# Shared experts as a loop of four groups of token tiles, with the last choice of experts ahead of it

## The chip, the cores and the metric

The kernel runs on one core of one Trainium2 chip. The metric is the device time in microseconds (us) of that core. Five engines work side by side: PE (matrix products), DVE (vector operations and reductions), ACT (activation functions and copies), POOL (here mainly transfers that go through a list of addresses) and SP (here only issues transfers). They run their own instruction lists and meet only at semaphores.

## The reference, cut to what matters

One transformer layer with adaptive norms: latent attention over 2048 tokens, then a mixture of experts of 32 routed experts, six per token, and two shared ones that every token goes through. The change lies in the second half:

```python
scores = jax.nn.sigmoid(x @ gate_w)
...
_, selected_experts = jax.lax.top_k(masked_scores, K)
weights = jnp.take_along_axis(original_scores, selected_experts, axis=-1)
weights = weights / jnp.sum(weights, axis=-1, keepdims=True)
...
g = jax.lax.ragged_dot(xs, w_gate, group_sizes)
u = jax.lax.ragged_dot(xs, w_up, group_sizes)
d = jax.lax.ragged_dot(jax.nn.silu(g) * u, w_down, group_sizes)
...
expert_out = jnp.sum(out * weights[..., None], axis=1)
shared = jax.nn.silu(x @ sw_gate) * (x @ sw_up) @ sw_down
return (expert_out + shared).reshape(B, S, H)
```

## The kernel before, in words

`attention` fills the first 1730 us and is untouched. `mixture` then works on 16 tiles of 128 tokens, in three stages that follow each other on PE.

**Token tiles.** For each tile PE projects the attention output (L1398), DVE adds it to x (`token_tile`, L1159) and normalizes (L1169), PE turns the tile (L1407), ACT modulates it into `h2T` (L1075), and PE computes the 32 scores (L1417). A choice of experts is made for a group of tiles at once: `choose` (L1179 to L1219) and `count_group` on DVE, `positions` on PE (L1430 to L1436), and `place` on DVE, which writes the list of slots (L1249). `GROUP` sets the groups: tiles 0 to 1, 2 to 7 and 8 to 15. The first two are chosen inside the loop over tiles, one and two tiles after the last tile of the group. When a group's slots stand, POOL scatters the rows of its tiles to the regions of the experts in DRAM, six transfers for each tile (L1050). One group's row of transfers is called a burst below: 12, 36 and 48 of them.

**Shared experts.** 32 units (16 tiles times the two halves of the shared experts), written out one after the other. In a unit PE computes gate and up (`shared_gate`, L1475), ACT the silu (L1103), DVE the product (L1313), PE turns it (`shared_turn`, L1484), ACT copies it (`shared_hidden`, L1109), PE multiplies down (`shared_down`, L1493); after each second unit DVE adds the result to x (L1339). The gate product of unit n+2 is issued ahead of the down product of unit n. The choice of the last group is spread between the first six units; `count_chosen`, `tile_table` (L1253 to L1274), `spread_table` (L1448) and `keep_table` follow up to unit 10. They yield the table that says which expert each of the 128 routed tiles uses; SP waits for it before it loads the first weights (L1008). `weigh_tokens` (L1285 to L1293), seven pieces on DVE, is spread over units 12 to 24.

**Routed experts.** 128 tiles, a loop on every engine with eight tiles in its body: SP loads a tile's weights (L1008, one transfer of 608 KB) and its rows (L1014), PE, ACT and DVE do the same steps as for a unit (L1519 to L1542, product on DVE L1348), POOL scatters the result (L1059). `combine` then adds six rows per token to x (L1611).

```python
GROUP = ((0, 2), (2, 8), (8, 16))
...
for n in range(UNITS):
    shared_turn(n)
    if n + 2 < UNITS:
        shared_gate(n + 2)
    shared_down(n)
```

Of the kernel before, what the change touches and what calls it, by code (L numbers as in the profile page):

```python
# [36 lines left out]
TOPK = 6  # L37
GROUPS = 4
EPG = E // GROUPS
M = 176  # L40
# [830 lines left out]
def mixture(nc, a, x, ident, mod, wov, cbar, routing, weight, slots_dram, ranked_dram):  # L871

    st = ExitStack()
    with st:
# [24 lines left out]
        h2T = sb("h2T", T * D)  # L899
# [71 lines left out]
        folded = sem("folded3")  # L971
        sg_mm = sem("sg_mm3")
# [22 lines left out]
        CREDIT = {r_mm: U, r_used: 2, g_mm: 2, hid_ready: 2, h_mm: 2, h_used: 2, y_mm: U, y_ready: 2}  # L995
# [70 lines left out]
        def _(act):  # L1066
# [32 lines left out]
            def shared_silu(n):  # L1099
                act.wait_ge(sg_mm, n + 1)  # L1100
                if n >= 2:
                    act.wait_ge(s_hid, n - 1)
                act.activation(ex[n % 2][:, :], p_g[n % 2][:, 0:M], ACT.Silu).then_inc(s_silued, 1)  # L1103

            def shared_hidden(n):
                act.wait_ge(sh_mm, n + 1)
                if n >= 2:
                    act.wait_ge(sd_mm, n - 1)
# [44 lines left out]
        def _(v):  # L1153
# [155 lines left out]
            def shared_hid(n):  # L1309
                v.wait_ge(s_silued, n + 1)  # L1310
                if n >= 2:
                    v.wait_ge(sh_mm, n - 1)
                v.tensor_tensor(hid[n % 2][:, :], ex[n % 2][:, :], p_g[n % 2][:, M:2 * M], ALU.mult).then_inc(s_hid, 1)  # L1313

            for n in range(2):
                shared_hid(n)
            for n in range(UNITS):
                if n + 2 < UNITS:
                    shared_hid(n + 2)
                if n == 0:  # L1320
                    scores(END)
                if n == 1:
                    best_groups(END)
                if n == 2:
                    inside_groups(END)
                if n == 3:
                    best_experts(END)
                if n == 4:
                    count_group(END)
                if n == 5:  # L1330
                    place(END)
                if n == 7:
                    tile_table()
                if n == 10:
                    keep_table()
                if n % 2 == 1:
                    t = n // 2
                    v.wait_ge(sd_mm, n + 1)
                    v.tensor_tensor(x[:, t * D:(t + 1) * D], p_y[t % 2][:, 0:D], x[:, t * D:(t + 1) * D],  # L1339
                                    ALU.add).then_inc(s_added, 1)  # L1340
                if n % 2 == 0 and 12 <= n < 12 + 2 * (TOPK + 1):
                    weigh_tokens((n - 14) // 2)
# [41 lines left out]
        def _(pe):  # L1384
# [85 lines left out]
            def shared_gate(n):  # L1470
                t = n // 2
                if n >= 2:
                    pe.wait_ge(s_hid, n - 1)
# [5 lines left out]
            def shared_turn(n):  # L1479
                pe.wait_ge(s_hid, n + 1)  # L1480
                if n >= 2:
                    pe.wait_ge(sh_used, n - 1)
# [4 lines left out]
            def shared_down(n):  # L1487
                t = n // 2
                pe.wait_ge(sh_used, n + 1)
                if n % 2 == 0 and t >= 2:  # L1490
                    pe.wait_ge(s_added, t - 1)
                for k in range(2):
                    last = pe.matmul(p_y[t % 2][:, 0:D], hidT[n % 2][:, k * P:(k + 1) * P],  # L1493
# [3 lines left out]

            pe.wait_ge(ld_ws, 32)
            pe.wait_ge(folded, 2)
            for n in range(2):  # L1500
                shared_gate(n)
            pe.wait_ge(x_used, T)
            for n in range(UNITS):
                shared_turn(n)
                if n + 2 < UNITS:
                    shared_gate(n + 2)
                shared_down(n)
                if n == 4:
                    positions(END)
                if n == 5:  # L1510
                    count_chosen()
                if n == 9:
                    spread_table()
# [43 lines left out]
            pe.wait_ge(s_added, T)  # L1557
# [122 lines left out]
```

## Time and profile before

| what | value |
|---|---|
| median of 3 runs | 2381.33 us (2379.02 to 2386.78) |
| the profiled execution's own time | 2386.19 us |
| its span, first to last instruction | 2384.4 us |
| busy share of the span | PE 90%, DVE 63%, ACT 58%, POOL 56% |
| attention ends, token tiles begin | about 1733 us into the span |
| last addition of the shared experts | 1987.39 us |
| first and last scatter issue (L1050) | 1759.2 and 1936.0 us |
| first transfer of results to be combined lands | about 2334 us |

Times in the rows are microseconds from the start of the span. In a row of the timeline the first number is the start and the second the duration; what stands in brackets is how long the engine sat idle before it, and who released it. "remote" there means that the profile found no event of another engine close before the release. PE and its weight loads (PEld) are listed apart; a product of 32-bit floats shows as two matmuls for each one of the code. `x4` counts instructions that were merged into a row. The granted clock is 1.00 at the higher level of TensorE's clock and 0.50 at the lower.

### The profile page before, as it was taken

How to read it: one execution, taken by the hardware profiler on the slowest of the kernel's cores; microseconds unless marked ns; L12 is line 12 of the kernel's file. 1: busy time of each engine (PE TensorE's matmuls, PEld its weight loads, DVE VectorE, ACT ScalarE, POOL GpSimd, SP SyncE). 2: the span in 40 equal slices, each digit the busy share in tenths (PEclk: the TensorE clock that was granted, in tenths of full speed). 3: DMA queues.
4: the chain of work that ended last, by engine and by line, in shares of the span. 5: the costliest groups of instructions: out<-in, count | busy, mean ns of one | idle time of the engine just before them, and what ended most of it. 6: DMA issues, size and time to landing. Idle time of an engine off the chain costs nothing. (4 is left out here: it accounts for less than half of the span.)

```text
span 2384.4 us, 38677 instructions
## 1 busy us (share of the span) xinstructions
PE 2140.0 (90%) x10554; PEld 1421.9 (60%) x10554; DVE 1511.3 (63%) x3046; ACT 1375.4 (58%) x1927; POOL 1338.5 (56%) x762
## 2 busy tenths in 40 slices
PE   5896999999999999999999999999873659999990
PEld 3643666666666666666666666666553436777760
DVE  4536777777777777777777777777142324555557
ACT  2521677777777777777777777767731214555540
POOL 1001777777777777777777777777725331333330
PEclk8886999999999999999999999999986879999995
DMA  4119990000000000000000000000012244999987
GB/s 158 53 29 370 402 396 7 0 0 0 0 0 0 0 0 0 0 0 0 0 0 0 0 0 0 0 0 1 1 49 81 67 145 142 337 357 343 345 281 249
DMA packets 90336, 227.35 MB, mean 95 GB/s; under 512 B 13198, under 2 KB 46904, under 8 KB 90040
## 3 DMA queue, kind: packets, MB, share of 16 engines
q1 hardware_dynamic: 77240, 195.03, 23.1%
q0 software_dynamic: 10752, 29.72, 3.3%
q10 hardware_dynamic: 2304, 2.10, 0.3%
q8 instruction: 21, 0.34, 0.1%
q14 instruction: 19, 0.16, 0.0%
HBM read 125.52 MB, written 101.28 MB: 95 GB/s over the span
## 5 line engine op out<-in xcount | busy, mean ns | idle before, releaser
L632 POOL TENSOR_TENSOR prob_lo<-prob,prob_hi 128x1024 f16<-128x1024 f32 x512 | 1108.3, 2176 | 435.8 <-ACT prob_hi L651 425.8
L649 ACT ACTIVATE prob<-p_s,prob_scale 128x1024 f32<-128x1024 f32 x512 | 571.4, 1116 | 463.2 <-PE p_s L798 456.9
L684 DVE TENSOR_REDUCE maxes<-p_m 128x1 f32<-128x512 f32 x1024 | 700.7, 691 | 120.5 <-PE p_m L771 103.8
L651 ACT ACTIVATE prob_hi<-p_s,prob_scale 128x1024 f16<-128x1024 f32 x512 | 567.3, 1108 | 0.0
L771 PE MATMUL p_m<-k_hi,q_hi 96*128 96x512 f32 x1024 | 420.5, 414 | 10.4 <-DVE maxes L684 7.7
L798 PE MATMUL p_s<-q_hi,k_hi 97*128 97x512 f32 x1024 | 360.0, 433 | 5.5 <-ACT prob_hi L651 3.9
L798 PE MATMUL p_s<-q_lo,k_hi 97*128 97x512 f32 x1024 | 323.6, 397 | 0.0
L798 PE MATMUL p_s<-q_hi,k_lo 97*128 97x512 f32 x1024 | 323.1, 397 | 0.0
L1059 POOL DMA_INDIRECT ranked_out<-y,dest x128 | 122.8, 959 | 265.7 <-DVE y L1363 258.4
L771 PEld LDWEIGHTS p_m<-k_hi,q_hi 96*128 96x128 f32 x1024 | 195.4, 191 | 91.4 <-DVE maxes L684 34.8
L798 PEld LDWEIGHTS p_s<-q_hi,k_hi 97*128 97x128 f32 x1024 | 171.4, 189 | 121.2 <-issue 67.9
L798 PEld LDWEIGHTS p_s<-q_lo,k_hi 97*128 97x128 f32 x1024 | 192.2, 190 | 41.2 <-issue 1.0
L798 PEld LDWEIGHTS p_s<-q_hi,k_lo 97*128 97x128 f32 x1024 | 192.4, 190 | 40.5
L811 PE MATMUL p_o<-prob_hi,c_hi 128*64 128x512 f16 x1024 | 199.1, 386 | 2.9 <-POOL prob_lo L632 2.9
L811 PE MATMUL p_o<-prob_hi,c_lo 128*64 128x512 f16 x1024 | 196.0, 379 | 0.0
L811 PE MATMUL p_o<-prob_lo,c_hi 128*64 128x512 f16 x1024 | 196.0, 379 | 0.0
L1527 PE MATMUL bank<-w,rT 128*128 128x352 f32 x512 | 175.4, 466 | 2.1 <-ACT rT L1075 2.1
L1050 POOL DMA_INDIRECT expert_rows<-hall,slot x96 | 92.5, 964 | 104.3 <-DVE slot L1249 75.9
L1542 PE MATMUL bank<-w,hidT 88*128 88x256 f32 x512 | 131.9, 379 | 0.9 <-ACT hidT L1131 0.9
L1348 DVE TENSOR_TENSOR hid<-ex,bank 128x176 f32<-128x176 f32 x128 | 43.2, 338 | 134.4 <-ACT ex L1126 124.3
L761 PE MATMUL p_x<-hT,wq 128*96 128x512 f32 x256 | 123.1, 603 | 5.4 <-POOL q_lo L624 3.0
L673 DVE TENSOR_TENSOR q_raw<-p_x,cosq 96x512 f32<-96x512 f32 x64 | 43.9, 687 | 126.3 <-PE p_x L761 126.3
(231 smaller groups left out, 2259.0 us busy)
## 6 DMA issues: line engine op xcount, KB each, us to landing
w<-in_experts SPq DMA_DIRECT2D x128, 608.0 KB
expert_rows<-zeros SPq DMA_DIRECT2D x129, 526.0 KB, 9.1
rows<-expert_rows SPq DMA_DIRECT2D x128, 131.5 KB
got<-ranked_out SPq DMA_DIRECT2D x16, 768.0 KB, 11.1
wqb<-in_wqb SPq DMA_DIRECT2D x16, 341.0 KB, 3.0
x<-in_x SPq DMA_DIRECT2D x1, 2048.0 KB, 8.5
cbar<-in_woT SPq DMA_DIRECT2D x1, 2048.0 KB
ranked_out<-y,dest POOLq DMA_INDIRECT x128
```

Of the source, the lines that this page charges most:

```text
L632: gp.tensor_tensor(prob_lo[s % NB][:, :], prob[s % 2][:, :], prob_hi[s % NB][:, :], ALU.subtract).then_inc(lo_ready, 1)
L649: act.activation(prob[s % 2][:, :], p_s[s % 2][:, :], ACT.Exp, bias=prob_scale[:, :], scale=SCALE)
L651: act.activation(prob_hi[s % NB][:, :], p_s[s % 2][:, :], ACT.Exp, bias=prob_scale[:, :], scale=SCALE).then_inc(p_ready, 1)
L684: v.tensor_reduce(maxes[:, n:n + 1], p_m[n % 2][:, :], AX.X, ALU.max).then_inc(max_used, 1)
L761: last = pe.matmul(p_x[0:KA, :], wq[:, k * KA:(k + 1) * KA], hT[:, k * S + c * QC:k * S + (c + 1) * QC], start=(k == 0), stop=(k == DK - 1))
L771: pe.matmul(p_m[n % 2][:, :], q_hi[half][0:KA, j * P:(j + 1) * P], k_hi[0:KA, kc * QC:(kc + 1) * QC], start=True, stop=True).then_inc(max_ ...
L798: last = pe.matmul(p_s[kt % 2][:, j * QC:(j + 1) * QC], kk[0:KS, keys], qq[half][0:KS, j * QC:(j + 1) * QC], start=(part == 0), stop=(part ...
L811: last = pe.matmul(p_o[j * CP:(j + 1) * CP, :], cc[:, kt * CP:(kt + 1) * CP], pp[:, j * QC:(j + 1) * QC], start=(kt == 0 and part == 0), s ...
L1050: gp.indirect_dma_start(out=slots_dram[0:E * S, :], out_offset=bass.IndirectOffsetOnAxis(ap=slot[:, t * 8 + j:t * 8 + j + 1], axis=0), in_ ...
L1059: gp.indirect_dma_start(out=ranked_dram, out_offset=bass.IndirectOffsetOnAxis(ap=dest[u][:, :], axis=0), in_=y[u][:, :], in_offset=None).t ...
L1527: last = pe.matmul(p_g[u % 2][:, 0:2 * M], rT[u % 2][:, k * P:(k + 1) * P], w[u % U][:, k * 2 * M:(k + 1) * 2 * M], start=(k == 0), stop=( ...
L1542: last = pe.matmul(p_y[u % 2][:, 0:D], hidT[u % 2][:, k * P:(k + 1) * P], w[u % U][0:MH, WIN + k * D:WIN + (k + 1) * D], start=(k == 0), s ...
```

## The change

The groups of tiles become 0 to 5, 6 to 11 and 12 to 15, so the bursts have 36, 36 and 24 transfers, and the first two choices come at tiles 7 and 13 instead of 3 and 9. The choice of the last group, the table of tiles and its spreading stand ahead of the shared experts on DVE and PE. The shared experts become a loop of four trips on PE, ACT and DVE; a trip has eight units (four token tiles). [...] All seven pieces of `weigh_tokens` stand behind the loop on DVE, ahead of the first product of the routed tiles. Semaphores of the stage start with a credit of two, so that a wait in the loop never is for zero. The weights of a tile are loaded by one transfer in both kernels; the diff has no line on them.

```diff
-        UNITS = 2 * T
+        ST = 4
+        UNITS = 2 * ST
-        GROUP = ((0, 2), (2, 8), (8, 16))
+        GROUP = ((0, 6), (6, 12), (12, 16))
...
@@ scalar
+            def copy_h(q, tl):
+                act.wait_ge(sg_mm, q * UNITS + 2 * max(tl - 2, -1) + 4)
+                act.copy(rT[tl % 2][:, :], h2T[:, ds((q * ST + tl) * D, D)]).then_inc(rc_ready, 1)
...
-            for n in range(2):
-                shared_silu(n)
-            for n in range(UNITS):
-                shared_hidden(n)
-                if n + 2 < UNITS:
-                    shared_silu(n + 2)
+            with act.Fori(0, T // ST) as q:
+                for n in range(2):
+                    copy_h(q, n)
+                for n in range(2):
+                    shared_silu(q, n)
+                for n in range(UNITS):
+                    shared_hidden(q, n)
+                    if n % 2 == 0 and n // 2 + 2 < ST:
+                        copy_h(q, n // 2 + 2)
+                    if n + 2 < UNITS:
+                        shared_silu(q, n + 2)
...
@@ vector
+            choose(END)
+            count_group(END)
+            place(END)
+            tile_table()
+            keep_table()
...
-            for n in range(2):
-                shared_hid(n)
-            for n in range(UNITS):
-                if n + 2 < UNITS:
-                    shared_hid(n + 2)
-                if n == 0:
-                    scores(END)
...
-                if n % 2 == 0 and 12 <= n < 12 + 2 * (TOPK + 1):
-                    weigh_tokens((n - 14) // 2)
+            with v.Fori(0, T // ST) as q:
+                for n in range(2):
+                    shared_hid(q, n)
+                for n in range(UNITS):
+                    if n + 2 < UNITS:
+                        shared_hid(q, n + 2)
+                    if n % 2 == 1:
+                        xt = x[:, ds((q * ST + n // 2) * D, D)]
+                        v.wait_ge(sd_mm, q * UNITS + n + 3)
+                        v.tensor_tensor(xt, p_y[n // 2 % 2][:, 0:D], xt, ALU.add).then_inc(s_added, 1)
+            for j in range(-1, TOPK):
+                weigh_tokens(j)
...
@@ tensor
-            def shared_gate(n):
+            def shared_gate(q, n):
+                pe.wait_ge(rc_ready, q * ST + n // 2 + 3)
+                pe.wait_ge(s_hid, q * UNITS + n + 1)
...
-                    last = pe.matmul(p_g[n % 2][:, 0:2 * M], h2T[:, t * D + k * P:t * D + (k + 1) * P],
+                    last = pe.matmul(p_g[n % 2][:, 0:2 * M], rT[n // 2 % 2][:, k * P:(k + 1) * P],
...
+            positions(END)
+            count_chosen()
+            spread_table()
             pe.wait_ge(ld_ws, 32)
             pe.wait_ge(folded, 2)
-            for n in range(2):
-                shared_gate(n)
             pe.wait_ge(x_used, T)
-            for n in range(UNITS):
...
-                if n == 4:
-                    positions(END)
-                if n == 5:
-                    count_chosen()
-                if n == 9:
-                    spread_table()
+            with pe.Fori(0, T // ST) as q:
+                for n in range(2):
+                    shared_gate(q, n)
+                for n in range(UNITS):
+                    shared_turn(q, n)
+                    if n + 2 < UNITS:
+                        shared_gate(q, n + 2)
+                    shared_down(q, n)
```

How PE's list reads around the last group's positions. Before, they stand between the down product of unit 4 and the turn of unit 5 (L1430 to L1436 are `positions`, L1484 the turn, L1475 gate and up, L1493 down, L1443 `count_chosen`):

```order
L1493 MATMUL bank<-ws,hidT 128x256
L1430 MATMUL bank<-chosen,lower 128x256 [waits before_ready3,slots_ready3,chosen_ready3,pads3]
L1433 MATMUL bank<-chosen,ones 128x224
...
L1436 MATMUL bank<-chosen_before,ones 128x256
L1484 MATMUL bank<-ident,hid 88x128 [waits sh_used3,s_hid3]
...
L1493 MATMUL bank<-ws,hidT 128x256 [waits sh_used3]
L1493 MATMUL bank<-ws,hidT 128x256
L1443 MATMUL bank<-chosen_before,ones 128x32 [waits sc_ready3,before_ready3]
```

In the changed kernel (L1472 is gate and up, L1480 the turn):

```order
L1415 MATMUL bank<-gate,h2T 128x32
L1428 MATMUL bank<-chosen,lower 128x128 [waits before_ready3,slots_ready3,chosen_ready3,pads3]
...
L1434 MATMUL bank<-chosen_before,ones 128x128
L1441 MATMUL bank<-chosen_before,ones 128x32 [waits sc_ready3,before_ready3]
L1446 MATMUL bank<-spread,ones 128x256 [waits spread_ready3]
L1498 UNCONDITIONAL_BRANCH [waits x_used3,folded3,ld_ws3]
L1498 ISA
L1470 ISA [waits rc_ready3]
L1472 MATMUL bank<-ws,rT 128x352 [waits s_hid3]
```

All of the last choice and of the table now comes behind the last scores (L1415) and ahead of the first shared product.

DVE's list at the step from the shared to the routed experts, before (L1313 is a unit's product, L1291 to L1293 one piece of the weighing, L1339 the addition to x, L1348 a routed tile's product):

```order
L1313 TENSOR_TENSOR hid<-ex,bank 128x176 [waits sh_mm3,s_silued3]
L1291 TENSOR_TENSOR pick<-val,vtop 128x512
L1292 TENSOR_TENSOR pick<-pick,wn 128x512 [waits vec3]
L1293 TENSOR_REDUCE weight<-pick 128x16 [waits vec3]
L1313 TENSOR_TENSOR hid<-ex,bank 128x176 [waits sh_mm3,s_silued3,vec3]
...
L1339 TENSOR_TENSOR x<-bank,x 128x256 [waits sd_mm3] x2
L1348 TENSOR_TENSOR hid<-ex,bank 128x176 [waits h_mm,silued] x3
```

In the changed kernel (L1338 is the addition, L1294 to L1297 the first piece, L1346 the routed product):

```order
L1338 TENSOR_TENSOR x<-bank,x 128x256
L1329 REGISTER_ALU
L1329 COMPARE_AND_BRANCH
L1294 TENSOR_TENSOR wn<-sc,chosen 128x512
L1295 TENSOR_REDUCE wsum<-wn 128x16 [waits vec3]
L1296 RECIPROCAL wsum<-wsum 128x16 [waits vec3]
L1297 TENSOR_TENSOR wn<-wn,wsum 128x512 [waits vec3]
L1300 TENSOR_TENSOR pick<-val,vtop 128x512 [waits vec3]
...
L1302 TENSOR_REDUCE weight<-pick 128x16 [waits vec3]
L1346 TENSOR_TENSOR hid<-ex,bank 128x176 [waits h_mm,silued,vec3]
```

The weighing has moved out from between the units to a place where nothing of the shared experts is left, and the first routed product stands behind it.

## Rows read from the trace of the kernel before

**Rows 1.** Busy us (instructions) in stretches: PE, PEld, DVE, ACT, POOL; clock, DMA

```profile
1820.00:1840.00 20.00, 1.54 (x6) 1.14 (x6) 1.77 (x6) 0.90 (x3) 15.13 (x17) 0.50 0.30 104
1920.00:1940.00 20.00, 2.63 (x7) 2.10 (x8) 0.77 (x2) 0.69 (x2) 13.04 (x14) 0.50 0.51 166
2000.00:2020.00 20.00, 20.00 (x98) 15.22 (x97) 11.04 (x47) 11.21 (x34) 7.68 (x8) 1.00 0.93 323
```

**Rows 2.** Scatter transfers of POOL: all of them (ns), then single issues

```profile
L1050 POOL DMA_INDIRECT expert_rows<-hall,slot x96: 956/960/1176, 1759.2 to 1936.0; - x96
...
1800.27 1.07 POOL L1050 DMA_INDIRECT expert_rows<-hall,slot  x1 [25.99 <-DVE slot L1249]
...
1844.66 0.96 POOL L1050 DMA_INDIRECT expert_rows<-hall,slot  x1 [0.30 <-issue]
1876.58 0.96 POOL L1050 DMA_INDIRECT expert_rows<-hall,slot  x1 [30.96 <-DVE slot L1249]
```

**Rows 3.** Timeline, second burst: start, us, engine, line, operation, idle before

```profile
1808.81 0.81 ACT L1075 ACTIVATE h2T<-bank,mcol 128x128 f32<-128x128 f32 x2 [3.60 <-remote]
...
1821.51 0.81 ACT L1075 ACTIVATE h2T<-bank,mcol 128x128 f32<-128x128 f32 x2 [10.57 <-remote]
...
1848.87 0.81 ACT L1075 ACTIVATE h2T<-bank,mcol 128x128 f32<-128x128 f32 x2 [26.45 <-remote]
...
1823.25 0.67 PE L1407 MATMUL bank<-ident,hall 128*128 128x128 f32 x2
```

**Rows 4.** Timeline in the third burst, ACT, PE and the queue of SP

```profile
1908.95 0.37 ACT L1109 COPY hidT<-bank 88x256 f32<-88x256 f32 x1 [12.28 <-remote]
...
1943.96 0.32 ACT L1103 ACTIVATE ex<-bank 128x176 f32<-128x176 f32 x1 [6.64 <-remote]
...
1892.24 0.64 PE L1484 MATMUL bank<-ident,hid 128*88 128x128 f32 x2
...
1899.81 45.55 SPq L1008 DMA_DIRECT2D w<-in_experts  x8
```

**Rows 5.** Timeline of DVE at the first and at the second choice

```profile
1743.57 0.42 DVE L1159 TENSOR_TENSOR x<-bank,x 128x256 f32<-128x256 f32 x1
...
1746.36 0.42 DVE L1159 TENSOR_TENSOR x<-bank,x 128x256 f32<-128x256 f32 x1
...
1749.93 0.20 DVE L1179 TENSOR_SCALAR sc<-sc 128x64 f32<-128x64 f32 x1 [2.28 <-ACT sc L1095]
...
1784.63 0.26 DVE L1179 TENSOR_SCALAR sc<-sc 128x192 f32<-128x192 f32 x1 [2.84 <-ACT sc L1095]
...
1799.81 0.18 DVE L1249 TENSOR_SCALAR slot<-vtop 128x36 uint32<-128x36 f32 x1
```

**Rows 6.** Timeline at the table of tiles, DVE and PE

```profile
1879.20 0.68 DVE L1253 TENSOR_TENSOR tmp<-bank,limits 128x512 f32<-128x512 f32 x1
...
1885.54 0.70 PE L1448 MATMUL bank<-spread,ones 128*128 128x256 f32 x2 [1.58 <-issue]
```

**Rows 7.** Timeline at the end of the shared experts, PE and DVE

```profile
1979.25 1.35 PE L1475 MATMUL bank<-ws,h2T 128*128 128x352 f32 x4
...
1981.52 1.35 PE L1475 MATMUL bank<-ws,h2T 128*128 128x352 f32 x4
...
1986.22 1.13 PE L1493 MATMUL bank<-ws,hidT 88*128 88x256 f32 x4 [0.46 <-ACT hidT L1109]
...
1987.39 0.42 DVE L1339 TENSOR_TENSOR x<-bank,x 128x256 f32<-128x256 f32 x1 [3.19 <-PE bank L1493]
```

**Rows 8.** Timeline of DVE, first and last operation of a piece of weighing

```profile
1953.98 0.68 DVE L1291 TENSOR_TENSOR pick<-val,vtop 128x512 f32<-128x512 f32 x1
...
1955.43 0.69 DVE L1293 TENSOR_REDUCE weight<-pick 128x16 f32<-128x512 f32 x1
```

**Rows 9.** Timeline at the start of the routed tiles, DVE and PE

```profile
1992.08 0.34 DVE L1348 TENSOR_TENSOR hid<-ex,bank 128x176 f32<-128x176 f32 x1 [4.27 <-ACT ex L1126]
...
1995.95 0.57 PE L1535 MATMUL bank<-ident,hid 128*88 128x128 f32 x2
```

More of the change, by code:

```diff
@@ L971, in mixture @@
         folded = sem("folded3")
+        rc_ready = sem("rc_ready3")
         sg_mm = sem("sg_mm3")
@@ L1097, in _, with shared_silu, shared_hidden @@
             act.preload_act_table(ACT.Silu)
[L1099 to L1102, printed above, removed]
+            def copy_h(q, tl):
+                act.wait_ge(sg_mm, q * UNITS + 2 * max(tl - 2, -1) + 4)
+                act.copy(rT[tl % 2][:, :], h2T[:, ds((q * ST + tl) * D, D)]).then_inc(rc_ready, 1)
+            def shared_silu(q, n):
+                act.wait_ge(sg_mm, q * UNITS + n + 3)
+                act.wait_ge(s_hid, q * UNITS + n + 1)
                 act.activation(ex[n % 2][:, :], p_g[n % 2][:, 0:M], ACT.Silu).then_inc(s_silued, 1)
[L1105 to L1108, printed above, removed]
+            def shared_hidden(q, n):
+                act.wait_ge(sh_mm, q * UNITS + n + 3)
+                act.wait_ge(sd_mm, q * UNITS + n + 1)
                 act.copy(hidT[n % 2][:, :], p_h[n % 2][0:MH, 0:2 * P]).then_inc(sh_used, 1)
-            for n in range(2):
-                shared_silu(n)
-            for n in range(UNITS):
-                shared_hidden(n)
-                if n + 2 < UNITS:
-                    shared_silu(n + 2)
+            with act.Fori(0, T // ST) as q:
[9 more added lines that the diff above has]
+                        shared_silu(q, n + 2)
             def copy_rows(n, u):
@@ L1308, in _, with shared_hid @@
                         place(g)
[L1309 to L1312, printed above, removed]
-                v.tensor_tensor(hid[n % 2][:, :], ex[n % 2][:, :], p_g[n % 2][:, M:2 * M], ALU.mult).then_inc(s_hid, 1)
-            for n in range(2):
-                shared_hid(n)
-            for n in range(UNITS):
-                if n + 2 < UNITS:
-                    shared_hid(n + 2)
-                if n == 0:
-                    scores(END)
[L1322 to L1327, printed above, removed]
-                if n == 4:
-                    count_group(END)
-                if n == 5:
[L1331 to L1340, printed above, removed]
-                if n % 2 == 0 and 12 <= n < 12 + 2 * (TOPK + 1):
-                    weigh_tokens((n - 14) // 2)
+            choose(END)
[3 more added lines that the diff above has]
+            keep_table()
+            def shared_hid(q, n):
+                v.wait_ge(s_silued, q * UNITS + n + 1)
+                v.wait_ge(sh_mm, q * UNITS + n + 1)
+                v.tensor_tensor(hid[n % 2][:, :], ex[n % 2][:, :], p_g[n % 2][:, M:2 * M], ALU.mult).then_inc(s_hid, 1)
+            with v.Fori(0, T // ST) as q:
[10 more added lines that the diff above has]
+                weigh_tokens(j)
             def silu(n, u):
@@ L1468, in _, with shared_turn @@
                         positions(g)
-            def shared_gate(n):
-                t = n // 2
-                if n >= 2:
-                    pe.wait_ge(s_hid, n - 1)
+            def shared_gate(q, n):
+                pe.wait_ge(rc_ready, q * ST + n // 2 + 3)
+                pe.wait_ge(s_hid, q * UNITS + n + 1)
                 for k in range(DK):
-                    last = pe.matmul(p_g[n % 2][:, 0:2 * M], h2T[:, t * D + k * P:t * D + (k + 1) * P],
+                    last = pe.matmul(p_g[n % 2][:, 0:2 * M], rT[n // 2 % 2][:, k * P:(k + 1) * P],
                                      ws[n % 2][:, k * 2 * M:(k + 1) * 2 * M], start=(k == 0), stop=(k == DK - 1))
                 last.then_inc(sg_mm, 1)
[L1479 to L1482, printed above, removed]
+            def shared_turn(q, n):
+                pe.wait_ge(s_hid, q * UNITS + n + 3)
+                pe.wait_ge(sh_used, q * UNITS + n + 1)
                 for k in range(2):
@@ L1485, in shared_turn, with shared_down @@
                 last.then_inc(sh_mm, 1)
[L1487 to L1491, printed above, removed]
+            def shared_down(q, n):
+                pe.wait_ge(sh_used, q * UNITS + n + 3)
+                pe.wait_ge(s_added, q * ST + n // 2 + 1)
                 for k in range(2):
-                    last = pe.matmul(p_y[t % 2][:, 0:D], hidT[n % 2][:, k * P:(k + 1) * P],
+                    last = pe.matmul(p_y[n // 2 % 2][:, 0:D], hidT[n % 2][:, k * P:(k + 1) * P],
                                      ws[n % 2][0:MH, WIN + k * D:WIN + (k + 1) * D], start=(n % 2 == 0 and k == 0),
@@ L1556, in _ @@
             pe.wait_ge(tables, 2)
-            pe.wait_ge(s_added, T)
+            pe.wait_ge(s_added, T + 2)
             turn_rows(0, 0, 16)
```

8 lines of the change are left out of this document (1 added, 7 removed).

## The prediction

> **What bounds the kernel now.** I read the busy shares by stretch first, since one average covers three different stages. In the routed stage PE is busy 20.00 of 20.00 us at the full clock from 2000 to 2020 [rows 1]: whatever delays its start delays the end by the same amount. The stage ahead of it is another matter: from 1820 to 1840 PE is busy 1.54 us, from 1920 to 1940 2.63 us, at the low clock, while POOL is busy 13 to 15 us [rows 1].
>
> Then I asked what POOL does there. Its 96 scatter transfers [rows 2] come in three bursts. In the second, 35 steps take 1844.66 - 1800.27 = 44.4 us, 1.27 us each; the bursts run from 1759.2, from 1800.3 to 1845.6 and from 1876.6 to 1937.0. Nobody needs the rows yet: they are read only behind the shared experts, at 1987. But look at what others do in a burst. PE ends the turn of a tile at 1823.25 + 0.67 = 1823.9, and ACT, which waits for just that, starts at 1848.87, after 26.45 us of idling [rows 3]. PE ends a unit's turn at 1892.9, ACT copies it at 1908.95 [rows 4]. Such idling is marked "remote": no event stands near the release. SP needs 45.55 us to issue eight loads [rows 4]. So **in a burst, word from PE comes late**, by 10 to 25 us. It starts some 8.5 us into a burst (first late step 1808.81, burst from 1800.27 [rows 2, 3]) and ends 3 us after the second (1848.87 against 1845.6) and 7 us after the third (1943.96 against 1937.0) [rows 2 to 4]. The token tiles and the shared experts therefore stand almost still for 40 us in the second burst and 58 us in the third. Free of it, a unit takes 1981.52 - 1979.25 = 2.27 us [rows 7], bound by PE.
>
> **The change, part by part.** Bursts become 36, 36 and 24; their sum, 96 x 1.27 = 122 us, stays. What counts is when the last one ends and how much is left to do.
>
> *First burst.* Tiles come every 1746.36 - 1743.57 = 2.79 us. The first choice, four tiles later, starts at 1749.93 + 4 x 2.79 = 1761.1. From there to the end of its slots, six tiles took 1799.99 - 1784.63 = 15.4 us [rows 5]. The burst runs from 1776.8 to 1822.4.
>
> *Second burst.* The second burst of before also had 36 transfers, so its course can be laid over: the tile modulated at 1821.51, 21.2 us into the burst [rows 3], is now tile 12, at 1798. A further wait for PE (about 8 us in a burst, an estimate from the 12 us between 1808.81 and 1821.51) puts the scores on DVE near 1807. The choice of six ends at 1815, its positions come back from PE only when the burst is over, at 1822.4 + 3 = 1826. Placing adds 2 to 3 us: second burst from 1829 to 1874.6.
>
> *Third burst.* In the pause tile 15 is finished (about 9 us, three tile steps), then four tiles are chosen on DVE, about 6 us: 1841. Positions, count, table (1879.20 to 1885.54 is 6.3 us [rows 6], a bit stretched there by units between) and its spreading need word from PE three times, in starvation again; I take 10 us each, and the table stands at 1871. The slots were ready before 1874.6, so the third burst follows at once, 24 x 1.27 = 30.5 us, to 1905; word is normal again at 1910. Hence 34 us earlier than before (1943.96), with the shared experts hardly begun.
>
> *The loop.* In a trip, three gate products start within 2.6 us, five follow at 2.27 us. From the last one to the next trip's first I take 1986.22 - 1981.52 = 4.7 us plus 0.9 us of the last down product's weight loads, 5.6 us [rows 7]: 2.6 + 5 x 2.27 + 5.6 = 19.6 us. Four trips are 78.5 us; without the three seams it would be 74.2. The copies into `rT` cost nothing: ACT is busy 0.37 + 0.32 us of a unit's 2.27 [rows 4]; without that cover each would add its 0.4 us. From 1871 to 1910, in starvation, before's rate (one unit in some 28 us) gives 1.4 units, 3 us of work. The last addition starts at 1910 + 78.5 - 3 = 1985.5, against 1987.39: **-1.9 us**.
>
> *Weighing.* One piece takes 1956.12 - 1953.98 = 2.14 us [rows 8], the first an estimated 2.3 (three operations of that size, a small one): 15.1 us. Before, it lay between units on a DVE with room; now the cover is gone, and DVE's first routed product is behind it. PE's first turn, which needs that product, came 1995.95 - 1987.39 = 8.6 us after the start of the last addition [rows 7, 9]. It will come 0.4 + 15.1 + 0.4 = 15.9 us after it: +7.4. PE then starts anew at the low clock, where that turn takes 0.57 [rows 9]; the same turn took 0.64 at the low clock in the third burst [rows 4]: about +2. **+9.4 us**, with nothing behind it to catch up on a PE that is full.
>
> *Bounds.* No row shows the new course of the bursts. If the second abuts the first (slots by 1822), everything is 7 us earlier; if the second choice must wait until the first burst is over, it ends at 1826 + 15.4, and all is 13 us later. The weighing costs between 0 (routed stage held by something else) and 12.
>
> **Sum:** -1.9 + 9.4 = +7.5 us on the profiled execution's own 2386.19; that execution is 4.9 us above the median of 2381.33. Forecast: **2389 us**. A run of this kernel can tell about 0.3%, 7.1 us, from no change, so this sits at the edge.
>
> The routed loop already bears on what a branch costs: it branches back every eight tiles, and PE has no idle time there [rows 1]. I take zero for the seam itself. The Trainium skill ("Runtime: NRT & Kernel Launch", Instruction fetch mechanics) says that a taken branch whose target lies outside the two pages held forces a fetch, and that kernels had better be unrolled; by it the three branches would add time. By that rule, the trace of the routed loop disagrees.
>
> **The rivals.**
>
> *A, the forecast: 0.50*, 2380 to 2399.
>
> *B, the bursts abut: 0.17.* If word comes through sooner in the first burst, its 7 us gap goes: about 2381. For it: the first burst of before had only mild delays. Against: [rows 3].
>
> *C, the second choice comes only after the first burst: 0.10.* +13: 2402. The 26 us wait [rows 3] speaks for it.
>
> *D, the standstill is not of the scatter but of long written-out code: 0.10.* Then a loop runs free of it: table at 1871, 78.5 us of loop, 1950, instead of 1987: -37 + 9.4 gives about 2353. For it: "remote" names nobody, and even SP is slow. Against: the same written-out units run at 2.27 us once the burst is over [rows 7]. The Trainium skill ("SBUF — State Buffer", Who interferes with whom) says a DMA never contends with a compute engine, which would speak for this case. By that rule, the trace disagrees as far as it shows: ACT idles in the bursts alone.
>
> *E, the weighing is free: 0.08.* DMA is 93% busy in the routed stage [rows 1]; if it were the bound, the late start would be made good. Then 2380. Against: PE's 20.00 of 20.00.
>
> *F, the branch back costs a fetch: 0.05.* One that is as slow as a load's issue in a burst, 45.55 / 7 = 6.5 us [rows 4]: 2395.
>
> **How the numbers follow.** Faster than 2374.2: D and the low tails of A, B and E, 0.18. Within 7.1 us: most of B and E and A's lower part, 0.35. Slower than 2388.5: C, F and A's upper part, 0.47. The range reaches from 2368 to 2404: it holds A to C, E and F, with room for the burst's unknown course, and leaves out D.
>
> **What would show it right or wrong.** In the profile of the changed kernel: scatter issues from about 1777 to 1905 with at most one gap of some 7 us; the table (L1281 to L1288) inside the second burst; "remote" waits on ACT up to 1910 and none after; a gate product every 2.27 us with seams of 5.6 us; 15 us of L1294 to L1302 between the last L1338 and the first L1346, PE idle there for 7 us. It would be wrong if the loop ran at speed during a burst, if the last issue lay past 1920 or before 1895, or if PE waited for `rT`.

## The result and the profile after

The changed kernel takes **2413.62 us** (median of 4 runs, 2412.18 to 2415.70) where the kernel before took 2383.45 us (median of 4 runs, 2379.02 to 2386.78). The ratio is 1.0128, with a 95% interval from 1.0108 to 1.0149: slower by 30 us. The forecast was 2389, its range ended at 2404. The side was right, the size was not.

The profiled execution took 2412.18 us itself (span 2410.4), 26.0 us more than the one of before (2386.19). I read it in the order of the prediction. First busy time by stretch (the columns are those of [rows 1]), where PE works and where it does not:

```profile
1800.00:1820.00 20.00, 2.54 (x6) 1.46 (x5) 1.19 (x4) 0.00 (x0) 15.18 (x16) 0.50 0.30 108
...
1860.00:1880.00 20.00, 0.00 (x0) 0.00 (x0) 5.23 (x22) 0.00 (x0) 15.19 (x16) 0.50 0.30 108
1880.00:1900.00 20.00, 8.69 (x26) 5.16 (x26) 2.44 (x9) 1.31 (x4) 15.12 (x17) 0.78 0.39 138
1900.00:1920.00 20.00, 0.00 (x0) 0.00 (x0) 0.34 (x1) 0.32 (x1) 15.12 (x17) 0.56 0.55 173
...
1960.00:1980.00 20.00, 19.09 (x84) 13.75 (x83) 4.60 (x13) 6.84 (x21) 0.00 (x0) 1.00 0.00 0
```

In two stretches of 20 us PE does nothing at all, POOL issuing scatter transfers throughout. In the loop from 1940 to 2000 PE is busy 19.09 of 20 us at the full clock.

The scatter transfers, all of them and then the two that open a burst and the last one (timeline of POOL), answer to [rows 2]:

```profile
L1052 POOL DMA_INDIRECT expert_rows<-hall,slot x96: 956/960/1264, 1778.4 to 1919.7; - x96
...
1778.38 1.26 POOL L1052 DMA_INDIRECT expert_rows<-hall,slot  x1 [35.77 <-DVE slot L1258]
...
1844.87 1.07 POOL L1052 DMA_INDIRECT expert_rows<-hall,slot  x1 [20.93 <-DVE slot L1258]
...
1919.68 0.96 POOL L1052 DMA_INDIRECT expert_rows<-hall,slot  x1 [0.30 <-issue]
```

The first burst begins within 2 us of the forecast. Then comes one gap of 20.93 us, where I wrote 7, and all behind it is late. The second choice in the timelines of PE, ACT and DVE, which answers to [rows 3, 5], says why:

```profile
1797.59 0.69 PE L1405 MATMUL bank<-ident,hall 128*128 128x128 f32 x2 [2.99 <-issue]
...
1820.03 0.81 ACT L1077 ACTIVATE h2T<-bank,mcol 128x128 f32<-128x128 f32 x2 [23.14 <-remote]
1827.72 0.58 ACT L1073 COPY ctb<-bank 128x512 f32<-128x512 f32 x1 [6.89 <-remote]
...
1830.09 0.26 DVE L1188 TENSOR_SCALAR sc<-sc 128x192 f32<-128x192 f32 x1 [22.77 <-ACT sc L1097]
```

PE ends the turn of the tile at 1798.3. ACT, which waits for it, starts at 1820.03, still inside the first burst, and its next step waits until 1827.72. So the second choice's scores come at 1830.09, not at 1807.

The loop, by the last additions of its four trips, then the weighing and the first routed turn, which answer to [rows 7 to 9]:

```profile
1944.82 0.42 DVE L1338 TENSOR_TENSOR x<-bank,x 128x256 f32 x1 [3.19 <-PE bank L1487]
1964.43 0.42 DVE L1338 TENSOR_TENSOR x<-bank,x 128x256 f32 x1 [3.19 <-PE bank L1487]
1984.05 0.42 DVE L1338 TENSOR_TENSOR x<-bank,x 128x256 f32 x1 [3.19 <-PE bank L1487]
2003.66 0.42 DVE L1338 TENSOR_TENSOR x<-bank,x 128x256 f32 x1 [3.19 <-PE bank L1487]
2004.00 0.68 DVE L1294 TENSOR_TENSOR wn<-sc,chosen 128x512 f32<-128x512 f32 x1
2019.50 0.58 DVE L1346 TENSOR_TENSOR hid<-ex,bank 128x176 f32<-128x176 f32 x2
...
1923.23 2.07 PE L1487 MATMUL bank<-ws,hidT 88*128 88x256 f32 x4 [23.98 <-issue]
...
2019.97 0.65 PE L1527 MATMUL bank<-ident,hid 128*88 128x128 f32 x2 [7.30 <-DVE hid L1346]
```

The account of the 26.0 us between the two executions: the stage starts 1.9 us later (first addition of a token tile 1739.65 against 1737.77, ahead of everything that the change touches); the last shared addition, counted from there, comes 14.4 us later (264.0 against 249.6); the first routed turn follows it after 16.31 us and not 8.56, +7.75; from there to the end of the span 390.4 us pass and not 388.4, +2.0. These are 26.1. The last stretch takes 385.9 to 394.7 us in these two traces and the six taken below of kernels that show the late word or, as g1, run on such a chip, so its +2.0 alone proves little. What the low clock costs is read from the turns behind the first one: the second after it (2027.57) comes 7.60 us behind it, in the kernel before 5.75 us (2001.70 after 1995.95), +1.85.

### The profile page after: what moved, and what is told of

Same layout as the page of the kernel before. It is cut to its first block and busy times, and to the rows that moved or that the text cites. A ratio compares the mean times of both kernels' runs of the same rounds, so it can differ in the third digit from the quotient of the medians.

```text
span 2410.4 us, 38935 instructions
## 1 busy us (share of the span) xinstructions
PE 2141.2 (89%) x10554; PEld 1425.0 (59%) x10554; DVE 1511.7 (63%) x3046; ACT 1379.4 (57%) x1943; POOL 1339.0 (56%) x762
## 5 line engine op out<-in xcount | busy, mean ns | idle before, releaser
L771 PE MATMUL p_m<-k_hi,q_hi 96*128 96x512 f32 x1024 | 421.2, 414 | 10.4 <-DVE maxes L684 7.7
L798 PEld LDWEIGHTS p_s<-q_hi,k_hi 97*128 97x128 f32 x1024 | 171.3, 189 | 120.8 <-issue 67.9
L1346 DVE TENSOR_TENSOR hid<-ex,bank 128x176 f32<-128x176 f32 x128 | 43.1, 337 | 130.2 <-ACT ex L1135 115.2
```

The costliest lines, as they stand in the source:

```text
L771: pe.matmul(p_m[n % 2][:, :], q_hi[half][0:KA, j * P:(j + 1) * P], k_hi[0:KA, kc * QC:(kc + 1) * QC], start=True, stop=True).then_inc(max_ ...
L798: last = pe.matmul(p_s[kt % 2][:, j * QC:(j + 1) * QC], kk[0:KS, keys], qq[half][0:KS, j * QC:(j + 1) * QC], start=(part == 0), stop=(part ...
```

## The experiments

One fact ordered them. The runs came in jobs, each a sitting on one chip, and in some jobs the late word does not exist. The median of the kernel before is either 2383 to 2393 us or 2297 to 2300 us in a job, and the runs of one job all lie near one of the two. In the second case no trace has a single "remote" wait from 1740 on, with the same number of transfers. I call the chips of the first sort late chips, those of the second prompt chips; that it is the chip isn't shown (last section). The table gives from each trace the time from the first token tile's addition to the last shared one, and from there to the first routed turn (us):

| kernel, chip | first to last addition | to first turn |
|---|---|---|
| before, late | 249.6 | 8.6 |
| changed, late | 264.0 | 16.3 |
| g2_written_out, late | 262.8 | 16.3 |
| m1_new_groups, late | 248.1 | 5.9 |
| f2_before_four_groups, late | 243.8 | 5.9 |
| g1_no_scatter (changed), late | 171.3 | 16.3 |
| r2_before, prompt | 152.0 | 20.1 |
| r1_after, prompt | 171.9 | 16.3 |

The first column repeats within some 4 us: f1_weigh_behind, which is the kernel before up to the last addition, has 249.8 on another chip, and m2_four_groups, the same kernel as f2, 247.5.

### Is the late word of the scatter transfers?

**g1_no_scatter** (e2_no_scatter and r3_no_scatter are the same kernel):

```diff
-    gp.indirect_dma_start(out=slots_dram[0:E * S, :],
...
-        in_=hall[:, t * RW:(t + 1) * RW], in_offset=None).then_inc(scattered, 16)
+    gp.sem_inc(scattered, 16)
```

The experts' rows then stay zero, and a second edit lets the last stage read other rows of the results, as many bytes.

> The changed kernel without its 96 scatter transfers (L1052): the expert's rows keep the zeros that the kernel writes first, so the routed experts compute on zeros; all else is issued as before. The run is meant for a chip on which the kernel before takes 2383 to 2386. Theory (the late word from PE needs POOL's scatter transfers, and most of what such a chip adds comes from it): about 2316 there too, under the kernel before by 70 us, no wait of over 10 us on a remote word in ACT's or DVE's waits from 1740 on. Rival (that chip is slower for another reason, and the scatter transfers only happen to lie beside it): 2400 and the remote waits stay. Where the kernel before takes 2297 both want 2316 and the run tells nothing new.

Measured on a late chip: 2321.80 us, the kernel before 2393.06 (ratio 0.9711, 0.9682 to 0.9741), the changed kernel in the form of g2 2414.09. Taking the transfers out gives 92 us back, and the table above has all of it ahead of the last shared addition (171.3 against 262.8 us). On prompt chips it gave nothing: 2315.73 and 2316.71, one run each, the changed kernel 2316.52. So there computing on zeros gains nothing. The longest waits of ACT from 1740 to 2010 in g1 (us in total, times, longest) name no remote one:

```profile
ACT ex L1105 <- PE bank L1469: 43.2, 32, 17.3
ACT h2T L1074 <- PE bank L1402: 42.9, 16, 9.5
```

In the changed kernel, in the profile of the result, the same view has these:

```profile
ACT h2T L1077 <- PE bank L1405: 40.5, 14, 9.5
...
ACT h2T L1077 <- remote: 29.5, 2, 23.1
ACT hidT L1113 <- remote: 20.7, 2, 15.1
```

So the late word needs two things together, scatter transfers and such a chip. The Trainium skill ("SBUF — State Buffer", Who interferes with whom) says that a DMA never contends with a compute engine. On a late chip the measurement is against it as far as the effect goes: 92 us go when the transfers go. Which resource is shared they don't tell, nor whether it is POOL's issuing or the traffic of the transfers, since both were taken out together.

> The 96 scatter transfers of POOL are left out (the semaphore is counted up instead; the last stage then reads other rows of the results, as many bytes). Theory of the bursts (word from PE comes late because POOL issues scatter transfers): every wait named remote goes, the table stands near 1840, the last addition of the shared experts comes at about 1920 instead of 2003.7, the total is about 85 us less, 2325 to 2335 us. Rival (long lists of instructions that have to be fetched, or the serial order itself): the waits stay, under 15 us are gained, 2400 or more.

> The changed kernel without the 96 scatter transfers, again. If the chip shows the late word in r1_after: by my theory (POOL's scatter issues bring it about) this one is free of it, 2310 to 2330, some 85 to 100 us less than r1_after; if the late word comes from something else it stays near 2400. If the chip shows no late word at all: 2316, as the first time, and nothing is told apart.

On the prompt chips theory and rival could not part, so both runs tell only that the transfers as such cost nothing there.

### The loop and the groups

**g2_written_out** replaces the three hardware loops by written-out code in the same order:

```diff
-            with pe.Fori(0, T // ST) as q:
+            for q in range(T // ST):
```

> The changed kernel with its three hardware loops (choice tiles, shared trips) written out: the same instructions in the same order, without branches and registers. Theory (the loop costs nothing beyond the order that it fixes): the time of the changed kernel within 3 us, 2316 where the kernel before takes 2297 and 2413 where it takes 2383; trips 19.6 us apart. Rival (turning back in the loop costs PE, DVE and ACT a fetch and a branch at each of three seams, some 1 to 4 us each): 3 to 12 us less. That the code which is now longer is fetched from memory and stalls would show as more, by idle time ended by issue on PE or SP.

Measured: 2414.09 us (2413.76 to 2416.99), ratio 1.0096 (1.0065 to 1.0126) to the kernel before on that chip. Its trips, again by their last additions:

```profile
1965.43 0.42 DVE L1338 TENSOR_TENSOR x<-bank,x 128x256 f32<-128x256 f32 x1 [3.19 <-PE bank L1487]
1985.04 0.42 DVE L1338 TENSOR_TENSOR x<-bank,x 128x256 f32<-128x256 f32 x1 [3.19 <-PE bank L1487]
2004.65 0.42 DVE L1338 TENSOR_TENSOR x<-bank,x 128x256 f32<-128x256 f32 x1 [3.19 <-PE bank L1487]
```

They are 19.61 us apart, in the loop 19.61 as well: the seam is one of dependences, and turning back costs nothing that these rows show. The totals alone would not decide it: g2 lies 21 us above the kernel before of its own job, the changed kernel 30 us above that of its own (0.96% and 1.28%, their intervals overlap).

**m1_new_groups** (r4, h1 and k1 are the same kernel) is the kernel before with the groups of the change alone:

```diff
-        GROUP = ((0, 2), (2, 8), (8, 16))
+        GROUP = ((0, 6), (6, 12), (12, 16))
```

> Before with groups of 6, 6 and 4 tiles, as in k1_new_groups_again. Where the kernel before takes 2383 to 2393: 10 to 16 us over it if the groups bring the late second choice, within 4 us if the loop's order does. Where it takes 2297 to 2300: ratio 1.000 to 1.003.

> The kernel before with the token tiles in the groups of the change (6, 6, 4), nothing else. For a chip on which the kernel before takes 2383 to 2393. Theory (a first burst of 36 transfers stands over the word that the second choice needs, so its scores come at its end, about 1828, and all that follows is late by some 15 us): DVE's first scores of the second choice near 1828, last transfer near 1920, shared stage's last addition 10 to 16 us later than in the kernel before, total 10 to 16 us over it. Rival (the groups do no harm, it is the loop's order, in which no unit stands between the bursts): within 4 us of the kernel before. Where the kernel before takes 2297: ratio 1.003 again.

Measured on a late chip, as m1: 2390.17 us against 2392.06, ratio 0.9998 (0.9984 to 1.0012). (h1 itself fell on a prompt chip: 1.0000, 0.9987 to 1.0014.) My theory, that the groups bring the loss, fell. Yet its first step is there, as DVE's timeline of m1 shows:

```profile
1838.60 0.26 DVE L1179 TENSOR_SCALAR sc<-sc 128x192 f32<-128x192 f32 x1 [16.50 <-ACT sc L1095]
```

This execution starts its stage at 1746.25, 6.6 us later than the changed kernel's, and the scores are 8.5 us later: the second choice is late here too, by 1.9 us more. What differs is the filling. Here are the gate products of the shared units (four matmuls each) up to the last scatter transfer: of the kernel before, of m1, and of the changed kernel.

```profile
L1475 PE MATMUL bank<-ws,h2T x60: 459/459/934, 1853.0 to 1913.4; 128*128 128x352 f32 x60
```

```profile
L1475 PE MATMUL bank<-ws,h2T x56: 459/460/794, 1857.6 to 1932.0; 128*128 128x352 f32 x56
```

```profile
L1472 PE MATMUL bank<-ws,rT x16: 459/459/795, 1886.7 to 1898.8; 128*128 128x352 f32 x16
```

Of 32 units, 15 and 14 have started by the last transfer where units stand between the bursts, and 4 where the loop stands behind the table. The last transfer comes at 1936.0 in the kernel before, at 1941.7 in m1 and at 1919.7 in the changed one; but 17 units are left to start in the first, 18 in m1 and 28 here. Eleven units more at 2.27 us each are 25 us, more than the 16.3 that the last transfer comes sooner.

**h2_loop_old_groups** (e3_old_groups is the same) is the changed kernel with the old groups.

> The changed kernel with the old groups (2, 6, 8 tiles). For a chip on which the kernel before takes 2383 to 2393. Theory (the groups bring the 15 us): the second choice's scores come about 1785 as in the kernel before, the shared stage's last addition 10 us or more earlier than in the changed kernel (2003.7), total 2395 to 2403, what is left being the weighing of 9.7. Rival (the loop's order brings it, in which the third burst, now of 48 transfers, ends before any unit runs): last addition 2000 to 2010, total 2410 to 2416. Where the kernel before takes 2297: 2316 again.

> The changed kernel with the old groups of 2, 6 and 8 tiles (12, 36 and 48 transfers). By the theory of the bursts the third burst of 61 us starts only behind the choice of the last eight tiles, near 1870, and ends near 1931 (the changed kernel's ends at 1920.7); word is normal at about 1938; the loop's last addition comes near 2013, total 2422 to 2426 us. Rival (the new groups are what costs, since the first choice comes later and the second falls into a burst): 2385 to 2405 us.

Both fell on prompt chips: 2319.27 us (ratio 1.0097, 1.0073 to 1.0121) and 2316.23 (1.0070, 1.0045 to 1.0096), as the changed kernel there (1.0077). So on a prompt chip the groups don't matter in the loop either. On a late one this kernel wasn't measured; that the loop's order costs some 15 us there follows from m1 and g2 together, not from a run of that order alone.

> The kernel before with the groups of the changed kernel (6, 6 and 4 tiles), nothing else changed. The first burst starts at 1778 instead of 1759. Without the late word the 96 transfers run from 1778 without a gap to 1900, and the routed tiles start some 4 us later than before: 2298 to 2308 us. With the late word: the second burst starts near 1845, the third ends near 1921, word is normal near 1929 with three units done, total 2385 to 2400.

> Before with the token tiles in groups of 6, 6 and 4, nothing else, once more, in the hope of a chip on which the kernel before takes 2383 to 2393. Theory (groups bring it): DVE's first scores of the second choice near 1828, total 10 to 16 us over the kernel before. Rival (the loop's order brings it): within 4 us of the kernel before. Where the kernel before takes 2297 to 2300: ratio 1.000 to 1.003 again.

Ratios on prompt chips: 1.0028 (1.0015 to 1.0041) and 1.0026 (1.0009 to 1.0044). With h1 the groups cost there some 6 us in two jobs and nothing in a third.

### The weighing

**f1_weigh_behind** moves it behind the shared stage in the kernel before:

```diff
-                if n % 2 == 0 and 12 <= n < 12 + 2 * (TOPK + 1):
-                    weigh_tokens((n - 14) // 2)
...
+            for j in range(-1, TOPK):
+                weigh_tokens(j)
```

> Before, with all of the weighing (L1294 to L1302) moved behind the shared stage, nothing else. Theory (the kernel before starts its routed stage when the rows of the last scatter transfer land, 13.14 us after PE has run out of work in run r2_before, so that weighing there is hidden): 2297 within 6 us where this chip shows the kernel before at 2297, first turn of the routed experts still about 1908.8. Rival (weighing costs its 9.4 us wherever it stands behind the shared stage): 2306. Where this chip shows the kernel before at 2383, the theory wants 2393, because there PE waits for no rows ahead of the routed stage.

Measured on a late chip: 2400.55 us against 2386.01, ratio 1.0061 (1.0046 to 1.0075), +14.5 us where about 10 were expected. PE's timeline at the first routed turn:

```profile
2006.46 0.65 PE L1535 MATMUL bank<-ident,hid 128*88 128x128 f32 x2 [8.77 <-DVE hid L1348]
```

It comes 16.31 us after the last addition (1990.15), to the hundredth as in the changed kernel: +7.75 against the 8.56 of the kernel before. But that 8.56 has a loss in it. Its trace runs the first two routed gate products at the low clock (2.47 and 2.71 us, granted clock 0.50 from 1990 to 1995); m1, f2 and m2, with the same end of the shared stage, run them at the high one (1.45 us) and need 5.9 us. The second of these products, in the kernel before and in m1:

```profile
1993.02 2.71 PE L1527 MATMUL bank<-w,rT 128*128 128x352 f32 x4 [0.90 <-ACT rT L1075]
```

```profile
1998.69 1.45 PE L1527 MATMUL bank<-w,rT 128*128 128x352 f32 x4 [0.90 <-ACT rT L1075]
```

Against those three traces the weighing costs 10.4. Why the clock fell in the one trace and not in the three isn't shown.

From the first routed turn to the end pass 393.2 us, 4.8 more than in the kernel before. The low clock behind the wait explains some 2 of them: the second turn after the first comes 7.95 us behind it, against 5.75. The rest I can't place, in a stretch that varies by 8.8 us on late chips.

**e1_weigh_ahead** moves it in the changed kernel from behind the loop to behind the table:

> The seven pieces of weigh_tokens stand ahead of the loop on DVE, right behind keep_table, instead of behind it. My theory of that term: behind the loop they hold back the first routed product by 15.9 - 8.6 = 7.4 us and leave TensorE at its low clock, 9.7 us in all; ahead of the loop they fall into the third burst, where DVE idles, at a cost of 1 to 3 us. So 7 to 9 us less than the changed kernel: 2405 to 2407 us. Rival (the routed stage makes good for a late start): no difference, 2414.

Measured on a prompt chip: 2320.01 us, ratio 1.0091 (1.0061 to 1.0120), no better than behind the loop. The 15 us only changed their place in one serial chain. PE's first turn of a unit now waits 12.9 us for DVE's product, which stands behind them. The time from the first to the last addition grows from 171.9 to 186.3 us, and the time from there to the first routed turn shrinks from 16.3 to 5.9. Under the third burst of a late chip they might hide; that wasn't tried.

### What bounds a prompt chip

> The kernel before as it is, for a profile beside the changed kernel's. Without the late word I expect its routed stage to be held by the last scatter transfer (issue near 1896), not by the shared experts, so that what the changed kernel adds (choice and table in series, seams, weighing) costs it only what goes past that transfer: total 2290 to 2305. With the late word: 2379 to 2387.

> The changed kernel as it is, once more, since the last four kernels ran without any late word from PE (no wait named remote in their traces) and the kernel before took 2298 us beside them. If this chip is again without the late word: the loop's last addition near 1911 and the first routed turn 16 us behind it, span 2313 to 2316, total 2314 to 2318 us, some 18 us above the kernel before. If the late word is back: 2408 to 2418 us as at first.

The kernel before took 2293.71 us (2296.51 over 13 runs), the changed one 2316.52, ratio 1.0077 (1.0056 to 1.0098). So the change costs 18 to 20 us there too, and in another way. PE at the end of the shared stage, first in the kernel before, then in the changed one:

```profile
1901.76 0.66 PE L1519 MATMUL bank<-ident,rows 128*128 128x128 f32 x2 [13.14 <-DMA rows<-expert_rows]
...
1908.78 0.38 PE L1535 MATMUL bank<-ident,hid 128*88 128x128 f32 x2
```

```profile
1911.67 0.41 PE L1511 MATMUL bank<-ident,rows 128*128 128x128 f32 x2 [0.69 <-issue]
...
1927.46 0.65 PE L1527 MATMUL bank<-ident,hid 128*88 128x128 f32 x2 [8.77 <-DVE hid L1346]
```

The kernel before is out of work at 1888.7 and waits 13 us for rows that the last scatter transfer (1896.2) writes. The changed kernel waits for no rows; its additions end 22.5 us later (1911.15 against 1888.65), 2.7 of them because its stage starts later, the rest because its units start behind the table, at 1830.6 and not at 1804.8. Then comes the weighing. From its last addition to the first routed turn pass 16.3 us, in the kernel before, with its wait, 20.1. Together that is +18.7 us at the first turn.

**e4_paced** and **h3_paced** put two small fills of POOL behind each transfer of the changed kernel:

> The changed kernel with two small memsets on POOL behind every scatter transfer, which makes a step 1.8 us instead of 1.27. If the late word comes from how dense the issues are (something fills in the first 8 us of a burst), it becomes rare: the shared loop runs during the bursts, the end is set by the last transfer near 1950, total 2350 to 2370 us. If each transfer costs the others a fixed time, or POOL's issuing as such blocks them, nothing is gained, and the longer bursts cost up to 50 us: 2415 to 2460.

> The changed kernel with two small fills of POOL behind each scatter transfer, so that one starts every 1.75 us and not every 1.26. For a chip on which the kernel before takes 2383 to 2393. Theory (PE's word is late wherever POOL's scatter transfers follow one another, however dense): remote waits of over 10 us stay, the last transfer is at 1944 or later, total 2430 to 2445. Rival (with some room between two transfers the word gets through): no remote wait over 3 us, total 2346 as on a chip without the late word. Where the kernel before takes 2297: 2346 again.

Both fell on prompt chips, 2346.35 and 2348.72 us. The last transfer came at 1944.2 and 1946.5, and PE waited for its rows, as this line of e4 shows:

```profile
1949.77 0.66 PE L1514 MATMUL bank<-ident,rows 128*128 128x128 f32 x2 [39.69 <-DMA rows<-expert_rows]
```

So a last transfer that is late enough holds the routed stage of a prompt chip. Whether room between the transfers lets PE's word through stays open.

### Four groups, faster than both on late chips

**f2_before_four_groups** (m2_four_groups is the same kernel) gives the kernel before a small first group and four in all:

```diff
-        GROUP = ((0, 2), (2, 8), (8, 16))
+        GROUP = ((0, 2), (2, 6), (6, 11), (11, 16))
```

> Before, with its token tiles in groups 0 to 1, 2 to 5, 6 to 10 and 11 to 15 and nothing else changed. Theory (POOL idles for 35.1 us in two gaps of run r2_before, 18.7 ahead of its first scatter transfer and 16.4 between first and second burst, and its last transfer sets the routed stage's start): a small first group and a larger second one leave POOL with shorter gaps, the last transfer about 1887 instead of 1896.2, total 2287 to 2290 where the kernel before takes 2297. Rival (the last burst needs the last token tile's choice, which ends the same): 2297, no gain. Where the kernel before takes 2383 the theory has no number; a longer time than before would say that scatter transfers that start earlier cost more of PE's words.

> Before with groups of 2, 4, 5 and 5 tiles, as in f2_before_four_groups. Where the kernel before takes 2383 to 2393: 0.2 to 0.5% under it again. Where it takes 2297 to 2300, theory (the last scatter transfer sets the routed stage's start and comes about 9 us earlier): 2287 to 2290; rival (the last burst ends the same, the last choice being what it waits for): 2297.

Measured on two late chips: 2378.12 against 2386.01 us, ratio 0.9967 (0.9955 to 0.9979), and 2382.97 against 2392.06, 0.9959 (0.9944 to 0.9975). The transfers, all of them:

```profile
L1050 POOL DMA_INDIRECT expert_rows<-hall,slot x96: 957/963/1178, 1760.7 to 1930.5; - x96
```

They end 5.5 us earlier than in [rows 2], POOL's gaps are 68.8 us in total instead of 75.9, and the last shared addition is 5.8 us nearer to the first token tile. In m2 it is 2.2 us nearer (247.5), with the last transfer at 1934.1. The gain is small, 0.3 to 0.4%, but clear of no change in both jobs. On a prompt chip it wasn't measured, and neither was it run beside the changed kernel, which lies 1.0 to 1.3% above the kernel before on late chips.

## Why the prediction was wrong in size

**First burst: right.** Forecast from 1776.8, measured from 1778.38 with a start 1.9 us later.

**Second burst: this step failed.** I laid the second burst of [rows 3] over the new first one and took the milder of its two waits: "a further wait for PE (about 8 us in a burst, ...) puts the scores on DVE near 1807". The wait was 23.14 us, close to the 26.45 of the other row of that group, and a second one of 6.89 us followed it, up to 1827.72, when the burst had ended (1823.9). Scores were 23.1 us late, the second burst began at 1844.87 and not at 1829, and the last transfer came at 1919.68, not at 1903.8 (1905 less the last step): 15.9 us late, 1.9 of them start. This was rival C, "the second choice comes only after the first burst", priced at +13 and given 0.10. One burst had shown two waits, of 10 and of 26 us; I had no reason to give the lighter one five times the chance.

**Third burst and table: right in form.** No gap stands between second and third burst, the table is inside. PE got word again at 1923.23, 2.6 us after the end of the last transfer, where I had allowed 5. Before that it worked for a while inside the burst: four gate products went out between 1886.75 and 1899.3, then it stood for 23.98 us.

**Loop: trips right, ramp missed.** Trips of 19.61 us were forecast as 19.6. But from 1923.23 to the last addition 80.4 us pass, where 78.5 - 3 = 75.5 were forecast. The first trip's last addition comes 21.6 us after 1923.23, 5.0 more than the 19.6 - 3 that I allowed it: PE came out of the burst at the low clock (0.56 to 0.59 granted, down products of 2.07 and 1.91 us against 1.03), and of the four units with their gate products out one had its down product done. The copies into `rT` (`copy_h` in the diff), from which PE now reads a tile, cost nothing, as forecast: no wait of PE in the loop is for them. Together 13.2 + 4.9 = 18.1 us of the 18.2 by which the last addition (2003.66) missed 1985.5.

**Weighing: right.** 15.9 us from last addition to first turn were forecast, 16.31 came, and f1 shows the same 16.31 by itself. The 2 us for the low clock were put down without a sum; the turns behind it give 1.85. So +9.6 against +9.4, measured on the trace from which I forecast; against m1, f2 and m2, whose first turn comes 2.7 us sooner, it would be 12.

**Rivals.** B (the bursts abut) and E (weighing free) fell on the rows above. D, that the written-out code is to blame, fell by g2 (the same time without a loop) and by g1 (92 us back without transfers). F, that a branch back costs a fetch, fell by g2; I had also priced it at one fetch of 6.5 us where three seams would make 19.5, about 2408. The Trainium skill ("Runtime: NRT & Kernel Launch", Instruction fetch mechanics) charges a fetch only where the branch's target lies outside the two pages held. Whether these targets do, no run shows; the trips of 19.61 us in both forms show no charge.

**What I didn't see at all** is the chip. The whole argument rests on a starvation that half of the jobs don't show. The direction held on both sorts, by luck of two mechanisms: on a late chip too few units lie ahead of the last transfer, on a prompt chip the units start behind the table.

## What to carry to other kernels

When producers of one stage are moved ahead of filler work, count the filler that is still left when the slow resource lets go (here 28 units instead of 17), not only how early it lets go (here 16 us). Where the only trace shows two sizes of one wait, price the forecast by the larger one too, and give it its chance. And before a stall is built into a forecast, have the same kernel run on a second chip: a stall of 90 us was absent there.

## What the runs showed of the hardware

With 96 indirect transfers issued by POOL 1.26 us apart, ACT waited up to 28.8 us for word from PE in four of eight jobs (in m1, where PE had ended its turn 27.2 us before), and word was prompt in the other four; the kernel before took 2383 to 2393 us in the first and 2297 to 2300 us in the second. Three of the prompt jobs were on one and the same chip and the fourth on another, three late ones on three others, and the chip of the result above is not on record. So it looks like a property of the chip; that isn't shown, since no chip was seen in both sorts or often enough, and the mechanism is open. On a late chip the transfers cost the changed kernel 92 us, on a prompt one nothing.
